# Four-stage attention and feed-forward kernel on one core: the barrier between the first attention and the first feed-forward is taken out, and the head of the feed-forward is written into the attention's tiles

## What is computed

```
q, k, v  = projections of layernorm(x) and of the context, 16 heads of width 16
scores   = q k^T + mask ; attn = softmax(scores / 4)
x        = x + (attn v) Wo^T + bo

act_quant(x)    : s = 127 / max(|x| over the row) ; round(x * s) / s
weight_quant(w) : s = 1 / mean(|w| over the whole matrix) ; clip(round(w * s), -1, 1) / s
h = act_quant(z) weight_quant(w1)^T          (z = layernorm(x), 1024 hidden units)
h = depthwise convolution of h along the 256 positions, 3 taps, plus bias ; silu
x = x + act_quant(h) weight_quant(w2)^T
```

## Time and profile before

| | |
|---|---|
| Median of 3 runs | 1234.88 us (1233.9, 1234.88, 1239.96) |
| Profiled execution, its own time | 1232.73 us |
| Its span in the trace | 1231.0 us |
| PE, matmuls | 1111.4 us busy, 90% of the span |
| DVE | 751.2 us, 61% |
| POOL | 522.0 us, 42% |
| ACT | 428.1 us, 35% |
| Mean granted TensorE clock | 0.943 of full speed |
| Share of PE in the chain that ended last | 69% |

### The profile page before, as it was taken

One profiled execution on the slowest core, in us unless ns is written; L12 is line 12 of the kernel. 1 busy time (PEld: TensorE's weight loads), 2 busy tenths in 40 slices (PEclk: granted clock), 3 DMA queues, 4 the chain that ended last, 5 costly groups with the idle time before them and its releaser, 6 DMA issues.

```text
span 1231.0 us, 20861 instructions
## 1 busy us (share of the span) xinstructions
PE 1111.4 (90%) x7462; PEld 934.5 (76%) x7462; DVE 751.2 (61%) x1662; ACT 428.1 (35%) x882; POOL 522.0 (42%) x499
## 2 busy tenths in 40 slices
PE   6899799998899998999987999999997899968795
PEld 4688678886688855888987999999995688855564
DVE  2787779997688645888851222222226787636683
ACT  2455432333456511121112222222223356551475
POOL 4544503456477221667766110100364666420342
PEclk9999989999999989899977999999999899987898
DMA  7999400000200020000046332211212100000001
GB/s 275 386 387 387 150 1 1 23 1 1 83 1 1 1 97 0 1 2 26 27 142 237 110 113 95 103 38 38 85 51 57 44 1 1 1 1 0 1 26 43
DMA packets 43732, 93.59 MB, mean 76 GB/s; under 512 B 3821, under 2 KB 17806, under 8 KB 40838
## 3 DMA queue, kind: packets, MB, share of 16 engines
q1 hardware_dynamic: 35254, 62.24, 14.1%
q0 software_dynamic: 7104, 29.14, 6.6%
q10 hardware_dynamic: 1296, 1.18, 0.3%
HBM read 39.02 MB, written 51.51 MB: 74 GB/s over the span
## 4 chain that ended last, share of the span: by engine, by line
PE 69%; DVE 16%; ACT 5%; issue 4%; POOL 4%; DMA 1%; DVEq 0%; SPq 0%; POOLq 0%; ACTq 0%
PE PS L2153 11%; PE PS L2163 10%; PE PS L981 8%; PE PS L2030 4%; PE PS L1675 4%; PE PS L960 4%; PE PS L994 3%; PE PS L950 2%; PE PS L904 2%; PE PS L2019 2%; DVE scr L1174 2%; PE PS L1379 2%; DVE scr L1200 2%; PE PS L2056 1%; PE PS L901 1%
## 5 line engine op out<-in xcount | busy, mean ns | idle before, releaser
L2153 PEld LDWEIGHTS PS<-scr 128*128 128x128 f32 x992 | 118.2, 194 | 5.4 <-issue 1.7
L2153 PE MATMUL PS<-scr 128*128 128x128 f32 x992 | 120.3, 279 | 1.6 <-ACT scr L2181 1.3
L2186 ACT ACTIVATE scr<-PS,W 128x128 f32<-128x128 f32 x148 | 53.5, 367 | 192.6 <-PE PS L2153 192.6
L643 POOL TENSOR_TENSOR scr<-scr,small 128x1232 f32<-128x1232 f32 x32 | 71.8, 2245 | 102.3 <-DVE small L443 102.3
L2163 PE MATMUL PS<-scr 128*128 128x256 f32 x496 | 112.2, 379 | 0.0
L768 ACT ACTIVATE big<-PS 128x512 f32<-128x512 f32 x144 | 74.1, 524 | 85.8 <-PE PS L960 85.1
L2216 DVE TENSOR_SCALAR scr<-PS,W 128x128 f32<-128x128 f32 x148 | 51.3, 350 | 84.3 <-PE PS L2153 84.3
L2163 PEld LDWEIGHTS PS<-scr 128*128 128x128 f32 x496 | 91.8, 190 | 11.2
L2222 DVE TENSOR_TENSOR scr<-PS,W 128x256 f32<-128x256 f32 x37 | 15.7, 425 | 125.8 <-PE PS L2163 121.9
L960 PE MATMUL PS<-W,scr 128*128 128x128 f32 x480 | 78.8, 282 | 14.2 <-ACT scr L763 4.1
L981 PEld LDWEIGHTS PS<-scr,big 128*128 128x128 f32 x640 | 81.2, 191 | 6.8 <-issue 4.9
(11 more groups left out here) (410 smaller groups left out, 2488.2 us busy)
## 6 DMA issues: line engine op xcount, KB each, us to landing
expert_in<-zeros SPq DMA_DIRECT2D x1, 19712.0 KB, 55.7
expert_out<-zeros SPq DMA_DIRECT2D x1, 19712.0 KB, 106.9
scr<-ew_in POOLq DMA_DIRECT2D x12, 1024.0 KB, 6.4
scr<-expert_in SPq DMA_DIRECT2D x38, 128.0 KB, 2.0
big<-ew_in POOLq DMA_DIRECT2D x4, 1024.0 KB, 8.3
expert_out<-scr POOLq DMA_DIRECT2D x28, 128.0 KB, 2.0
W<-pack SPq DMA_DIRECT2D x1, 2458.0 KB, 8.6
W<-pack SPq DMA_DIRECT2D x1, 2152.0 KB, 9.4
```

The lines of the kernel that those rows point to most:

```text
L643: g.tensor_tensor(sc3, sc3, a_mx[u % 3].unsqueeze(2).broadcast_to([P, H, S2]), ALU.subtract).then_inc(s["sub_ready"], 1)
L2153: ins = pe.matmul(bank(1 + f % 4, G), e_w1[slot][:, k, f * P:(f + 1) * P], e_xT[:, k, :], start=(k == 0), stop=(k == C - 1))
L2186: a.activation(e_h[:, f, :], bank(1 + f % 4, G), ACT.Relu, bias=moe_bias(e, f)).then_inc(s["h_act"], 1)
```

## The change

- `stage_end("att0")` becomes `stage_left` on all four engines.
- **DVE**, in the attention's steps: the weight sums are cut into four halves (steps 3, 5, 7, 9); the statistics of sample 0 and 1 stand in steps 10 and 11; the totals are read from PSUM ahead of `scores(12)`; the means stand in step 11, the rounding of both weights and the normalised rows of sample 0 (`quant_rows`) in step 12, its scales (`quant_scales`) in step 13, its rounding (`quant_rounded`) in step 14, and in step 16 the first two products are kept. Everything extra stands between `normed(u - 1)` and `scores(u + 2)`.
- **POOL**: three taps in step 1, three in step 7, two in step 9, each behind `subtracted(u + 2)`; the two `ternary_rstd` in step 11, ahead of `subtracted(13)`. The next attention's zeroing is cut in four, one piece a sample for i from 1 to 4 of the feed-forward.
- **ACT**: the signs of the first weight in steps 12 and 13 (a half each), the copies of the turned sample 0 in step 15, and behind them the signs of the second weight, in front of the copy (`outs(15)`) for which PE's last projection waits.
- **PE**: the totals ahead of `scores(12)`, the turning of sample 0 between `projected(14)` and the last outputs of tile 15, the first product around `turned(15)`, and the second behind it.
- The tiles are cut so that these live beside the attention's: `f_w1q`, `f_zq`, `f_wide1`, `f_row1` go to `W1`, `f_z` and `f_zT` behind the attention's own cuts in `big`.

```diff
@@ att_dve, scores(u)
+                if lay == 0 and u == 12:
+                    totals_kept(v, ch)
@@ att_dve, steps
-                if lay == 0 and u in (14, 15):
-                    weight_sum(v, u - 14)
-                    ternary_stats(v, ch, u - 14)
+                if lay == 0 and u in (3, 5, 7, 9):
+                    weight_sum(v, (u - 3) // 4, (u - 3) // 2 % 2)
+                if lay == 0 and u == 10:
+                    ternary_stats(v, ch, 0)
+                if lay == 0 and u == 11:
+                    weight_means(v, ch)
+                    ternary_stats(v, ch, 1)
+                if lay == 0 and u == 12:
+                    weight_rounded(v, 0)
+                    weight_rounded(v, 1)
+                    quant_rows(v, ch, 0)
+                if lay == 0 and u == 13:
+                    quant_scales(v, ch)
+                if lay == 0 and u == 14:
+                    quant_rounded(v, ch)
                 if lay == 0 and u == NT:
-                    weight_means(v, ch)
-                    weight_rounded(v, 0)
+                    borders(v, ch, slice(0, PAIRS))
+                    ch.sync()
+                    first_kept(v, 0, (0, 1))
@@ att_pool
+        TAPS_AT = {1: (0, 1, 2), 7: (3, 4, 5), 9: (6, 7)}
+                if lay == 0 and u == 11:
+                    ternary_rstd(g, 0)
+                    ternary_rstd(g, 1)
                 if lay != 1 and u + 2 < NT:
                     subtracted(u + 2)
+                if lay == 0 and u in TAPS_AT:
+                    taps_made(g, TAPS_AT[u])
-            if lay == 0:
-                taps_made(g)
-                ternary_rstd(g, 0)
-                ternary_rstd(g, 1)
@@ att_act
+                if lay == 0 and u in (12, 13):
+                    first_signs(a, u - 12)
+                if lay == 0 and u == NT - 1:
+                    rows_turned(a, 0)
+                    second_signs(a)
@@ att_pe
+                if lay == 0 and u == NT:
+                    pe.wait_ge(ffn0["w_ready"], 2)
+                    pe.wait_ge(s["s_free"], S_FREE(0, NT - 1))
+                    first_made(pe, 0, 0)
                 if u >= 1:
                     turned(u - 1)
+                if lay == 0 and u == NT:
+                    first_made(pe, 0, 1)
+                if lay == 0 and u + 2 == 12:
+                    pe.wait_ge(s["s_free"], S_FREE(0, 11))
+                    weight_totals(pe)
...
+                if lay == 0 and u == NT - 1:
+                    pe.wait_ge(s["ring_free"], ring[0, "p", u, 1 if ring_bank(0, "p", u, 1) == 4 else 2] + 1)
+                    quantized_turned(pe, 0)
@@ ffn0_dve
-            ch.inc(v.tensor_scalar(f_mean127, f_mean, 1.0 / 127.0, None, ALU.mult))
-            ch.inc(v.memset(f_G[:, :, 0:1], 0.0))
-            ch.link(v.memset(f_G[:, :, S + 1:S + 2], 0.0))
-            quantized(0)
-            weight_rounded(v, 1)
-            hidden(0, range(PAIRS))
+            borders(v, ch, slice(PAIRS, FC))
+            ch.sync()
+            hidden(0, (2, 3))
@@ ffn0_pool
-            vb_zeroed(g, 1)
+                if i == 1:
+                    g.wait_ge(at_["o_full"], NT)
+                if 1 <= i <= 4:
+                    second_zeroed(i - 1)
@@ ffn0_act
-            weight_signs(a, 0)
-            normed(0)
-            weight_signs(a, 1)
@@ ffn0_pe
-            normed(0)
-            pe.wait_ge(s["w_ready"], 1)
-            for p in range(PAIRS):
-                hidden(0, p)
+            hidden(0, 2)
+            hidden(0, 3)
@@ the four engines
-            stage_end(v, "att0")
+            stage_left(v)
```

More of the change, by code:

```diff
@@ L1098, in ternary_stats, with weight_sum @@
             ins.then_inc(var_ready, 1)
-        def weight_sum(v, n):
-            if n == 0:
+        TOT_AT = 4 * S2
+        def weight_sum(v, n, c):
+            if n == 0 and c == 0:
                 v.wait_ge(in_ffn, 48)
@@ L1105, in weight_sum, with weight_totals @@
                 v.memset(f_round[:, 1:2], -ROUND)
-            v.tensor_reduce(f_tot[:, n:n + 1], (f_w1, f_w2)[n], AX.X, ALU.add,
+            half = (f_w1, f_w2)[n].rearrange("p (c n) -> p c n", c=C)[:, c, :]
+            v.tensor_reduce(f_tot[:, C * n + c:C * n + c + 1], half, AX.X, ALU.add,
                             apply_absolute_value=True).then_inc(ffn0["wsum_ready"], 1)
+        def weight_totals(pe):
+            pe.wait_ge(ffn0["wsum_ready"], 2 * C)
+            pe.matmul(bank(0, 2 * C, TOT_AT), ones, f_tot, start=True, stop=True)
@@ L1128, in taps_made, with first_signs, second_signs @@
+        def first_signs(a, c):
+            a.wait_ge(ffn0["w_rounded"], 1)
+            a.activation(f_w1q[:, c, :], f_w1[:, c * FF:(c + 1) * FF], ACT.Sign, bias=f_round[:, 1:2]).then_inc(ffn0["w_ready"], 1)
+        def second_signs(a):
+            a.wait_ge(ffn0["w_rounded"], 2)
+            a.activation(f_w2q.rearrange("p c n -> p (c n)"), f_w2, ACT.Sign, bias=f_round[:, 1:2]).then_inc(ffn0["w_ready"], 1)
+        def taps_made(g, fs):
             g.wait_ge(in_ffn, 48)
             taps = w["conv_w"].rearrange("p (f j) -> p f j", j=3)
-            for f in range(FC):
+            for f in fs:
@@ L1131, in taps_made, with quant_rows @@
                 g.tensor_tensor(f_taps[:, f, :, :], ident.unsqueeze(1).broadcast_to([P, 3, P]),
                                 taps[:, f, :].unsqueeze(2).broadcast_to([P, 3, P]), ALU.mult).then_inc(ffn0["taps_ready"], 1)
+        def quant_rows(v, ch, i):
+            b = i % 2
+            v.wait_ge(rstd_ready, i + 1)
+            for t in range(T):
+                ch.inc(v.tensor_scalar(f_z[:, t, :], X[:, T * i + t, :], f_mv[b][:, t, 0:1], f_rstd[b][:, t:t + 1],
+                                       ALU.subtract, ALU.mult))
@@ new lines, in quant_scales, with quant_rounded @@
+        def quant_scales(v, ch):
+            ch.sync()
+            ch.link(v.tensor_reduce(f_am, f_z[:, :, :], AX.X, ALU.max, apply_absolute_value=True))
+            ch.link(v.tensor_scalar(f_am, f_am, 1e-5, None, ALU.max))
+            ch.inc(v.tensor_scalar(f_deq, f_am, f_mean127[:, 0:1], None, ALU.mult))
+            ch.link(v.reciprocal(f_sc, f_am))
+            ch.link(v.tensor_scalar(f_sc, f_sc, 127.0, None, ALU.mult))
+        def quant_rounded(v, ch):
+            v.tensor_copy(f_wide1, f_deq.unsqueeze(2).broadcast_to([P, T, P])).then_inc(ffn0["wide1_ready"], 1)
+            for t in range(T):
+                ch.inc(v.tensor_scalar(f_z[:, t, :], f_z[:, t, :], f_sc[:, t:t + 1], ROUND, ALU.mult, ALU.add))
+            ch.sync()
+            v.tensor_scalar(f_zq, f_z[:, :, :], ROUND, None, ALU.subtract).then_inc(z_ready, T)
@@ new lines, in first_kept, with borders @@
+        def first_kept(v, i, pairs):
+            v.wait_ge(ffn0["zT_ready"], i + 1)
+            for p in pairs:
+                v.wait_ge(ffn0["h_psum"], PAIRS * i + p + 1)
+                v.tensor_tensor(f_G[:, 2 * p:2 * p + 2, 1:S + 1], bank(p % 2).rearrange("p (f s) -> p f s", f=2),
+                                f_row1.unsqueeze(1).broadcast_to([P, 2, S]), ALU.mult).then_inc(ffn0["g_ready"], 1)
+        def borders(v, ch, fs):
+            ch.inc(v.memset(f_G[:, fs, 0:1], 0.0))
+            ch.inc(v.memset(f_G[:, fs, S + 1:S + 2], 0.0))
@@ new lines, in rows_turned, with quantized_turned @@
+        def rows_turned(a, i):
+            a.wait_ge(ffn0["zT_psum"], i + 1)
+            if i:
+                a.wait_ge(ffn0["g_ready"], PAIRS * i)
+            a.activation(f_row1, bank(4, S, S), ACT.Copy)
+            a.activation(f_zT, bank(4).bitcast(BF16)[:, 0:C * S].rearrange("p (c s) -> p c s", c=C),
+                         ACT.Copy).then_inc(ffn0["zT_ready"], 1)
+        def quantized_turned(pe, i):
+            pe.wait_ge(z_ready, T * i + T)
+            pe.wait_ge(ffn0["wide1_ready"], i + 1)
+            if i:
+                pe.wait_ge(ffn0["zT_ready"], i)
+            for t in range(T):
+                pe.transpose(bank(4, P, S + t * P), f_wide1[:, t, :], ident)
+                for c in range(C):
+                    ins = pe.transpose(bank(4).bitcast(BF16)[:, c * S + t * P:c * S + (t + 1) * P],
+                                       f_zq[:, t, c * P:(c + 1) * P], identb[:, :])
+            ins.then_inc(ffn0["zT_psum"], 1)
@@ new lines, in first_made @@
+        def first_made(pe, i, p):
+            if p == 0:
+                pe.wait_ge(ffn0["zT_ready"], i + 1)
+            if i or p >= 2:
+                pe.wait_ge(ffn0["g_ready"], PAIRS * i + p - 1)
+            for f in (2 * p, 2 * p + 1):
+                for k in range(C):
+                    ins = pe.matmul(bank(p % 2, S, (f % 2) * S), f_w1q[:, k, f * P:(f + 1) * P], f_zT[:, k, :],
+                                    start=(k == 0), stop=(k == C - 1))
+            ins.then_inc(ffn0["h_psum"], 1)
```

99 lines of the change are left out of this document (28 added, 71 removed).

## The result

| | before | after |
|---|---|---|
| Median | 1234.99 us (8 runs, 1232.55 to 1239.96) | 1229.05 us (8 runs, 1227.63 to 1234.29) |
| Ratio, 95% interval | | 0.9952 (0.9933 to 0.9971) |
| Profiled execution, its own time | 1232.73 us | 1229.02 us |
| Span | 1231.0 us | 1227.3 us |
| First convolution starts, on the trace's axis | 160.99 us | 155.79 us |

The change gains 5.9 us by the medians, 0.48%. The last row but one is the measure used from here on: PE's first transpose of step 1, `turned(0)`, starts at 47.35 us before and 47.32 after, but some 2 us later in every experiment except number 5, so a plain start time would mix in what happened earlier. What happened is the clock: ahead of `turned(0)` PE waits 2.1 us for ACT in all fourteen profiles, and in eleven of them, all but before, after and number 5, the granted clock fell between 40 and 46 us.

The account below looks back on a forecast made before the run. PE was taken as the bound, with DVE close behind in the attention. A border gain of 11.5 us less 7.05 of attention costs gave 4.4: 1228.3 us profiled, 1230.5 as median, range 1224.5 to 1235.5.

Parts of the forecast that it names:

- The border: Between attention and first convolution: moved head and removed barrier start the convolution 11.2 us earlier, plus 0.3 from the clock.
- The taps: Attention steps 1, 7, 9: one POOL tap comes between DVE's two L390, 0.65 us a step, 1.95 in all.
- `gains` and totals: Attention: four small `gains` instructions in step 8 meet the last taps, 0.25 us; totals ahead of `scores(12)` cost 0.2.
- Step 11: Attention: DVE's means wait for POOL, L441 starts at about 120.6, no PE stall; tile 13's subtraction moves to 123.6.
- Step 12: Attention: DVE's rounding waits for POOL's subtraction and takes 2.5 us, `normed(12)` ends late, PE stalls 2.75 us.
- Step 13: Attention: DVE's scales wait for POOL's subtraction, then its bias; L441 starts at 136.45, PE stalls 1.9 us more.
- The clock: Rival: PE's clock falls once in the new attention stall, losing 2.3 us; gain 2.1, 1232.8 us; chance 0.17.
- forecast's own case: Whole kernel: costs and border gain as computed, a gain of 3 to 6 us; chance 0.42.
- first rival: Attention: small DVE instructions pass POOL unblocked, cost 1.0 instead of 4.65, gain 8.0 us, 1227; chance 0.34 including half of it.
- prediction's marks: Trace signs: convolution at about 156.8, L390 pairs about 3.1 us, PE waits for L453 about 2.7 and 1.9 us.
- slower: Rival: DVE behind POOL starves the attention by more than 11.5 us; 2.5 us slower, 1237.4; chance 0.05.
- The removed barrier changes nothing: Rival at the border: DVE's quantisation could still be late for PE, so no gain; chance 0.02.

Follow-up runs that it names:

- number 5: Changed kernel with ACT's signs of the second weight moved behind the copy that PE's last projection waits for: 1230.44 us, 0.9930 of before.
- second profile of after: The changed kernel run and profiled once more, unaltered, on another batch's chip: 1232.35 us, 0.9938 of before.
- number 6: Changed kernel with the barrier of all four engines put back behind the attention: 1235.13 us, 0.9964 of before.
- number 12: Changed kernel with taps, DVE's extra work and ACT's signs spread over other steps, plus the four-engine barrier put back: 1228.01 us; without that barrier 1227.94.
- number 4: Changed kernel with POOL's taps moved from steps 1, 7 and 9 to even steps 2 to 10: 1226.06 us, 0.9925 of before.
- number 2: Changed kernel with both weights' rounding and the first weight's signs moved to steps 14 and 15: 1222.76 us, 0.9919 of before.
- third batch: Four kernels on one chip with its own runs of before (1240.32 us); among them the changed kernel unaltered, 1232.35 us.
- number 8: Changed kernel with POOL's bias of the last sample moved from step 12 to behind step 13's subtraction: 1232.16 us, 0.9930 of before.

## Why the prediction was right, and where its terms were not

**The border, -11.5 us: right.** Of it 11.2 lie ahead of the convolution, where 11.23 were measured (20.38 to 9.15), and 0.3 behind it, for the clock. The wait for ACT's copy behind the second signs, 146.9 to 147.75 in the prediction, is 0.82 us in the row. The statement that nothing of the memset is paid again holds: the first of its pieces starts at 184.23 and takes 0.78 us, beside a reduction of DVE (183.65 to 185.58). From the first convolution to the end of the stage's last product the feed-forward takes 145.2 us (300.96 - 155.79), against 146.7 before (307.68 - 160.99), but those 1.5 us are not all the change's. About 1.0 of them is a fall of the clock near the stage's end, which the profile of before has (0.51 and 0.63 in two stretches of 2 us from 302 us) and that of after has not:

```profile
302.00:304.00 2.00, 1.50 (x4) 1.26 (x5) 1.97 (x3) 0.36 (x1) 2.00 (x1) 0.51 0.00 0
304.00:306.00 2.00, 2.00 (x9) 1.56 (x8) 1.78 (x4) 0.03 (x1) 2.00 (x1) 0.63 0.04 8
```

The second profile of after has such a fall too, from 296 us, and takes 146.15. So about 0.5 us (146.69 - 146.15) belong to the low clock at the start of the convolution, for which the working gave 0.3. The working put the gain on the barrier and the head together; numbers 6 and 12 split them: with the head moved, the barrier is worth 0.3 to 0.7 us, and the rest is the moved head.

**The taps, 1.95, with `gains` and totals 2.4: the way right, the size 1.36.** One line's instructions, apart (shortest, median and longest in ns, then the first and last start), L390 of before in step 7 and of after in step 1, and POOL's taps there:

```profile
L390 DVE TENSOR_SCALAR scr<-X,small x2: 401/1194/1987, 94.1 to 96.0; 128x256 f32<-128x256 f32 x2
```

```profile
L390 DVE TENSOR_SCALAR scr<-X,small x2: 917/1452/1987, 51.9 to 53.8; 128x256 f32<-128x256 f32 x2
...
L1179 POOL TENSOR_TENSOR W<-W x3: 821/870/877, 53.7 to 55.4; 128x384 f32<-128x384 f32 x3
```

The first L390 takes 1.99 us in both, until POOL's subtraction ends. The second takes 0.40 before and 0.92 after: a tap has started at 53.7, ahead of it, and takes some 0.87. So one tap comes between, as predicted. But part of it runs while the first L390 still does, and the pair grew by 0.52, not by 0.79. PE's delay up to `turned(10)` is 1.36 us; number 4 removes 1.24 of it, and the 0.12 that stay arise in step 10, where the totals stand (0.2 in the working). The four small instructions of `gains`, put at 0.25, cost PE nothing that can be told: one of them took 0.82 us beside a tap in place of 0.22, and from `turned(7)` to `turned(8)` the delay grew by 0.06 us, as it did from `turned(1)` to `turned(2)` without them. The Trainium skill, SBUF — State Buffer, "Who interferes with whom", says that a DVE instruction in a two-port mode contends with GpSimd: whoever issues first gets the shared port pair for the whole instruction, and the other is fully blocked. The trace agrees: the first L390 lasts until the subtraction ends. It adds how it went here with both queues filled: POOL's tap got in between DVE's two L390.

**Step 11, no stall: right.** The two means took 1.31 and 1.11 us and L443 of tile 13 started at 121.36, less 1.36 at 120.0, against 120.6. Part of that is a slip in the addition: the working's own terms (118.96 + 0.2, the small instruction's 0.2, and 1.0) give 120.4 at most. The subtraction of tile 13 came 0.65 us sooner than computed: 124.31, less the 1.36 by which the axis had moved, is 122.95, against 123.6.

**Step 12, stall 2.75: the term that was most mis-sized.** Measured 1.45 (2.81 - 1.36). The mechanism is the one predicted, the rounding waiting for the subtraction, and number 2 shows that it is the rounding that costs (1.68 us). The excess has four parts. The subtraction ended 0.65 earlier; the roundings were done 2.29 us behind it (128.84 - 126.55) in place of 2.5; the rows took 0.64 in place of 0.74; and the distance from the start of L443 to the end of `normed` is 133.25 - 129.40 = 3.85 us, not 4.10. The 4.10 came from a row in which DVE's residual L458 stood at 129.43, 0.14 behind the end of L443 (127.85 + 1.44) and just behind the end of PE's projection (128.23 + 1.09 = 129.32); in after it starts 0.09 ahead of that end, and the projection is long done. So the 4.10 held a short wait for PE and was not DVE's own time. These add up to 1.21 of the 1.30.

**Step 13, stall 1.9: mechanism right, size 1.39.** Both halves are in the rows: L1194 0.77 and L1195 1.19 us. From the bias's end to L443 it took 136.18 - 135.84 = 0.34 us, where the working has 136.45 - 135.62 = 0.83: that is 0.49 of the 0.51 by which it came out too high. By `turned(14)` 0.2 us come back.

**The clock.** The forecast left it out at the stalls, and gave it as a rival: one fall, 2.3 us. In the profile of after that rival happened, for 2.05 us, and the prediction's own mark for it, PEclk of 0.50 between 125 and 145 us, is in the stretch table; in the second profile of the same kernel it did not. The place and the price came out as given; that the wait is what lets the clock fall stays open. The chance of 0.17 was low for a fall that four of the six profiles with that wait show. The fall hid the oversized stalls: the attention lost 6.06 us in the profiled execution, against 7.05 computed, but 4.00 in the one without a fall. These are two errors of opposite sign, so that the profiled time came out within 1 us of the 1228.3 computed for it is in part luck.

**The sum.** Border 11.23, attention 6.06: 5.17 us for the profiled execution, where 11.2 - 7.05 = 4.15 were predicted up to the convolution and 4.4 in all. Without the fall the distance shortens by 7.22. The medians of the first result say 5.9, the third batch 8.0 (1240.32 - 1232.35). The forecast's own case, a gain of 3 to 6 us, thus holds in the first batch and not in the third, which comes out at the 8.0 of the first rival, though not by its mechanism. The prediction's marks come out the same way: the convolution at 155.79 (156.8 predicted), the pair of L390 at 2.83 us (about 3.1), nothing more lost from `turned(2)` to `turned(6)`, PE's wait for L453 of 1.40 where 2.7 was given, and none visible where 1.9 was. The span behind the convolution scatters by more than these differ (1071.5 us in after, 1076.0 in its second profile, 1070.0 before), so the end time alone could not have told the cases apart.

**The rivals.** *Small instructions are not blocked* falls: number 8 shows the same instruction with and without POOL beside it, 1.19 and 0.23 us. Its time, 1227, is yet nearly as near to the measured 1229.05 as the forecast of 1230.5, since the stalls were smaller for other reasons. The *slower* case needed 11.5 us lost between steps 1 and 14; 6.06 were, with one fall and not two. *The removed barrier changes nothing* falls as it was meant (DVE's quantisation was not late), though with the head moved the barrier alone is indeed next to nothing.

## What to carry to other kernels

When a barrier is taken out and work is moved ahead of it, cost the two apart: here the barrier was worth 0.3 to 0.7 us, the moved head over 10 at the border, for 4 to 6 lost where it was moved to. Extra DVE work goes where POOL is quiet: the same work in other steps, together with ACT's signs out of the way of the last copy, was worth another 4.65 us. And take an engine's own time between two instructions from a step in which it waited for nobody, or a hidden wait is counted as work. Before two profiles are subtracted, look where the clock fell in each: here falls at 41, 135, 154 or 302 us, 1 to 2.3 us each, were as large as the effects in question.

## What the runs showed of the hardware

- A `tensor_scalar` on DVE with two elements a partition took 0.77 to 1.31 us beside POOL's subtraction or bias, and one of them, 1.19 us beside the bias, took 0.23 with the bias moved away (number 8).
- With instructions queued on both sides, POOL's tap came between DVE's two L390: the second took 0.92 us in place of 0.40.
- TensorE's clock fell to 1.2 GHz behind a wait of 1.40 us in a stretch with dense work around it in four profiles of six, and in another execution of the same kernel it did not; behind the wait of 0.82 us in the tail it fell in two of eight, behind one of 2.1 us ahead of `turned(0)` in eleven of fourteen. A fall cost 2.05 us in step 13 and about 1.5 in the tail (107.96 against 106.42).
- A `stage_end` at which the engines arrive within a short time cost PE 0.70 us at full clock (number 12) and 0.28 in a tail with a fallen clock (number 6).
